# Edge counting with fewer TensorE transposes: x's row tiles 2 to 9 split into halves in rows and turned over by DMA

## The chip, the cores and the metric

The kernel runs as one program on one core of one Trainium2 chip. The metric is device time in microseconds of that core. All inputs start in HBM and the output ends there.

## What is computed

A graph of N = 1250 nodes and E = 41250 edges (`src`, `dst`, sorted by `dst`), node features `x` of 768 values. Three graph layers run one after another; the change touches the first one only. Cut to that layer:

```python
loop = arange(n);  src = concat(src, loop);  dst = concat(dst, loop)
deg = segment_sum(ones, dst)                       # edges into each node, self loop included
norm = rsqrt(deg)[src] * rsqrt(deg)[dst]
h = x @ W                                          # 1250 x 768 by 768 x 768
x = layernorm(x + segment_sum(h[src] * norm[:, None], dst) + b)
```

After it come two attention layers (4 heads of 256, then one head of 768), each with layer norm and a residual product, and a last layer norm.

## The kernel before, in words

**Tiling.** Nodes are cut into T = 10 row tiles of 128 (the last is padded). The program is written out for each engine by hand, with semaphores between them; there is no planner.

**The first layer as matrices.** The kernel doesn't gather edges. It counts them: a 1280 x 1280 matrix C of edge counts (source by destination) is built, and the aggregation is then a matrix product with C. In the same stretch TensorE computes h = x W0, piece by piece between counting blocks. Both factors are kept as a high and a low float16 half (`xt_hi`, `xt_lo`, `w0_hi`, `w0_lo`), and three of the four half products are added, so the product is nearly float32.

**Counting block b (80 of them, WD = 16 destinations each).** VectorE (`one_hots`, L1352) makes two one-hot operands, L1366 and L1367, in ring slot b % 4, so that it can be at most four blocks ahead of TensorE. TensorE (`count_block`, L813) starts the block with one matmul for the self loops (L821) and adds six matmuls (L828); the last of these gives the ring slot back. Then it runs the pieces of x W0 that `pieces_until` puts behind this block: a piece is one 128-wide slice k of one row tile t, and it has six matmuls (L776). From block 18 on there are 43 pieces for 62 blocks, so that 43 blocks have one piece and 19 have none (18, 21, 24, 27, 31, 34, 37, 40, 44, 47, 50, 53, 57, 60, 63, 66, 70, 73, 76). ScalarE copies the block's counts out of PSUM twice (L1103 and, by `cast` at L1068, `c_hi`) once TensorE has started what follows the counting matmuls of that block. After each eighth block TensorE also adds up degrees (`degrees`, L833, matmuls at L839). VectorE has two more steps in every eight blocks: `low_counts` (L1375) after block 8t+6 and the shift of the keys (L1386) after block 8t+4.

**x transposed.** The product needs x with features on partitions. For each row tile, TensorE transposes six 128 x 128 float32 blocks into PSUM buffer `p_out[t % 2]` (`transposes`, L729 to L738), ScalarE casts the result to `xt_hi` (`xt_high`, L1077, its cast at L1068), and VectorE subtracts this from PSUM into `xt_lo` (`xt_low`, L1341, at L1345). Tiles 0 and 1 are done before counting starts, their low half by TensorE and ScalarE too (`less_high`, `xt_rest`). Tiles 2 to 9 are done beside counting, in the blocks that `FETCH` names:

```python
FETCH = {done_block(t) + 2: t + 2 for t in range(T - 2)}
```

which is {13: 2, 19: 3, 28: 4, 37: 5, 45: 6, 54: 7, 63: 8, 71: 9} (block: tile). In such a block TensorE issues the transposes behind the block's pieces (L859), ScalarE casts behind the block's counts (L1105), and VectorE makes the low half after the one-hots of block b + FETCH_LAG, with FETCH_LAG = 4 (L1387). The first piece of tile t comes in block 19, 28, 36, 45, 54, 62, 71 and 79 for t = 2 to 9. The accumulator of tile t is `p_out[t % 2]` as well, so that the transposes wait until the product of tile t - 2 was copied out (`h_read`).

**After the last block.** Five pieces of tile 9 are held back (HELD = 5) and run behind the degrees. VectorE and GpSimd meanwhile turn the degrees into their inverse roots, ScalarE and VectorE scale h (L1116, L1408), and TensorE starts the aggregation (L885). SyncE's queue issued all loads of x and W0 in the first 12 us and then waits for `h_done` (L457) until W1's loads; nothing is on it during counting.

**DMA transposes elsewhere.** L463 (ten, each 128 rows by 1280 float16) and L518 (twenty, each 128 rows by 1024 float16) turn SBUF tiles over by DMA from SyncE's queue.

Of the kernel before, what the change touches and what calls it, by code (L numbers as in the profile page):

```python
# [17 lines left out]
P = 128  # L18
# [31 lines left out]
FETCH_LAG = 4  # L50
# [71 lines left out]
def gnn_program(nc, x, src, dst, W0, b0, W1, a_src1, a_dst1, b1, g1, be1, Wr1, br1,  # L122
# [7 lines left out]
    with ExitStack() as ctx:  # L130
# [102 lines left out]
        w0_lo = at(195 * KB, [KD, D], f16)  # L233
        src_i = at(156 * KB, [EG, P], i32)
# [120 lines left out]
        def everywhere(row):  # L355
# [7 lines left out]
            x_in0 x_in1 x_in2 x_in3 x_in4 x_in5 x_in6 x_in7 x_in8 x_in9 x_tr xt_hi_ok xt_lo_ok h_done h_read hs_hi_ok hs_lo_ok  # L363
# [66 lines left out]
        def _(sp):  # L430
# [18 lines left out]
            for t in range(T):  # L449
                if t == 2:  # L450
                    weights(0)
                if t < T - 1:
                    sp.dma_start(x_sb[:, t, :], x[t * P:(t + 1) * P, :]).then_inc(S[f"x_in{t}"], 16)
                else:
                    sp.wait_ge(S["pads"], 3)
                    sp.dma_start(x_sb[0:LAST, t, :], x[t * P:N, :]).then_inc(S[f"x_in{t}"], 16)
            sp.wait_ge(S["h_done"], T)  # L457
# [252 lines left out]
        def _(pe):  # L710
# [18 lines left out]
            def transposes(t):  # L729

                pe.wait_ge(S[f"x_in{t}"], 16)
                if t >= 2:
                    pe.wait_ge(S["h_read"], t - 1)
                else:
                    pe.wait_ge(S["ident_ok"], 4)
                for k in range(KD):
                    last = pe.transpose(p_out[t % 2][:, k * P:(k + 1) * P], x_sb[:, t, k * P:(k + 1) * P], ident)  # L737
                last.then_inc(S["x_tr"], 1)  # L738
# [63 lines left out]
            def project_nodes(t, k, counted=False):  # L802

                if k == 0:
                    pe.wait_ge(S["xt_lo_ok"], t + 1)
# [42 lines left out]
            for b in range(NB):  # L848
# [10 lines left out]
                if b in FETCH:  # L859
                    transposes(FETCH[b])  # L860
# [205 lines left out]
        def _(act):  # L1066
# [10 lines left out]
            def xt_high(t):  # L1077

                act.wait_ge(S["x_tr"], t + 1 if t < 2 else t + 3)
                cast(xt_hi[:, :, t * P:(t + 1) * P], p_out[t % 2].rearrange("p (k n) -> p k n", k=KD), S["xt_hi_ok"])  # L1080

            def xt_rest(t):

                act.wait_ge(S["x_tr"], t + 3)
                cast(xt_lo[:, :, t * P:(t + 1) * P], p_out[t % 2].rearrange("p (k n) -> p k n", k=KD), S["xt_lo_ok"])

# [12 lines left out]
            for b in range(NB):  # L1099
# [5 lines left out]
                if b in FETCH:  # L1105
                    xt_high(FETCH[b])
# [149 lines left out]
        def _(dve):  # L1256
# [84 lines left out]
            def xt_low(t):  # L1341

                dve.wait_ge(S["xt_hi_ok"], t + 1)
                cols = slice(t * P, (t + 1) * P)
                dve.tensor_tensor(xt_lo[:, :, cols], p_out[t % 2].rearrange("p (k n) -> p k n", k=KD), xt_hi[:, :, cols],  # L1345
                                  ALU.subtract).then_inc(S["xt_lo_ok"], 1)
# [30 lines left out]
            for b in range(NB):  # L1377
# [9 lines left out]
                if b - FETCH_LAG in FETCH:  # L1387
                    xt_low(FETCH[b - FETCH_LAG])
# [465 lines left out]
```

## Time and profile before

| | |
|---|---|
| time, median of 3 runs | 836.49 us (836.45 to 837.44) |
| the profiled execution's own time | 836.33 us |
| its span in the profile | 834.5 us |
| TensorE busy, VectorE busy, ScalarE busy | 807.4, 670.2, 269.2 us |
| mean granted TensorE clock | 0.997 of full speed |

How to read the profile: PE is TensorE's matmuls and PEld its weight loads, DVE is VectorE, ACT ScalarE, POOL GpSimd, SP SyncE; a q behind a name is that engine's sequencer. L828 is line 828 of the kernel. A timeline row has the start in us from the span's start, the time it took, the engine, the line, the operation and, in brackets, the idle time of the engine before it with what ended it. Matmuls overlap: the distance between two starts tells the pace, and the duration of one doesn't. The mean of 16 DMA engines' busy share stands at "DMA".

### The profile page before, as it was taken

What the parts mean: (1) busy time and instruction counts of PE and PEld (TensorE: products, weight loads), DVE (VectorE), ACT (ScalarE), POOL (GpSimd) and SP (SyncE); (2) the same over time, 40 slices, a digit from 0 to 9 for tenths busy, and PEclk for the clock granted to TensorE, in tenths of its full rate; (3) what the DMA queues carried; (4) which work ended last, traced back from release to release, by engine and by line L of the source; (5) the groups of instructions that cost most, each with busy time, mean ns of one, the idle gap of its engine ahead of it and who ended that gap; (6) DMA issues with size and microseconds to landing.
All of it is one profiled execution on the core that took longest, in us unless ns stands there. A gap on an engine that the chain in (4) does not pass through costs nothing.

```text
span 834.5 us, 13407 instructions
## 1 busy us (share of the span) xinstructions
PE 807.4 (97%) x4842; PEld 517.7 (62%) x4842; DVE 670.2 (80%) x1181; ACT 269.2 (32%) x509; POOL 58.8 (7%) x77
## 2 busy tenths in 40 slices
PE   5999999899999999999999999999999999999995
PEld 4566666466454444445888888885555666555552
DVE  7998885778666867998988899978893287996686
ACT  3444434510021101113555556645311108750000
POOL 3000002010203000000000000001111000001111
PEclk9999999999999999999999999999999999999998
DMA  8000002214741266215211322316756432112232
GB/s 309 7 2 2 1 2 70 103 50 157 148 93 70 76 238 225 83 75 207 86 51 50 108 58 89 113 58 143 174 127 157 158 114 76 58 58 76 76 114 72
DMA packets 58829, 82.06 MB, mean 98 GB/s; under 512 B 36997, under 2 KB 37997, under 8 KB 58639
## 3 DMA queue, kind: packets, MB, share of 16 engines
q1 hardware_dynamic: 57502, 76.13, 29.4%
q0 software_dynamic: 1264, 5.11, 1.9%
q8 instruction: 38, 0.62, 0.3%
q14 instruction: 25, 0.20, 0.1%
HBM read 52.40 MB, written 20.31 MB: 87 GB/s over the span
## 4 chain that ended last, share of the span: by engine, by line
PE 83%; DVE 9%; DMA 3%; SPq 2%; issue 2%; DVEq 1%; ACT 1%; POOL 0%; POOLq 0%
PE psum L980 21%; PE psum L962 19%; PE psum L1061 12%; PE psum L885 8%; PE psum L764 8%; DVE arena L1453 6%; PE psum L776 6%; PE psum L828 5%; SPq L463 2%; PE psum L821 1%; PE psum L737 1%; PE psum L992 1%; DMA arena<-as_scratch 1%; PE psum L839 1%; DMA arena<-uv_scratch 1%
## 5 line engine op out<-in xcount | busy, mean ns | idle before, releaser
L980 PE MATMUL psum<-arena 128*128 128x257 f32 x800 | 173.6, 380 | 1.0 <-DVE arena L1599 1.0
L980 PEld LDWEIGHTS psum<-arena 128*128 128x128 f32 x800 | 151.8, 190 | 22.9 <-issue 1.4
L764 PE MATMUL psum<-arena 128*128 128x512 f16 x720 | 158.4, 379 | 2.9 <-DVE arena L1425 1.9
L962 PE MATMUL psum<-arena 128*128 128x512 f16 x960 | 157.4, 326 | 0.0
L1068 ACT ACTIVATE arena<-psum 128x160 f16<-128x160 f32 (+5 forms) x178 | 83.1, 498 | 206.7 <-PE psum L764 73.7
L962 PEld LDWEIGHTS psum<-arena 128*128 128x128 f16 x960 | 93.6, 97 | 62.8
L764 PEld LDWEIGHTS psum<-arena 128*128 128x128 f16 x720 | 69.5, 98 | 88.4 <-issue 7.6
L1068 ACT ACTIVATE arena<-arena 128x1024 f16<-128x1024 f32 (+3 forms) x68 | 56.2, 842 | 135.5 <-DVE arena L1618 47.7
L1061 PE MATMUL psum<-arena 128*128 128x512 f16 (+2 forms) x600 | 98.4, 325 | 0.0
L1061 PEld LDWEIGHTS psum<-arena 128*128 128x128 f16 x600 | 58.3, 97 | 39.8
L1453 DVE CUSTOM_DVE_ANT_0 arena<-arena 128x1280 bf16<-128x1280 bf16 x50 | 71.0, 1489 | 14.9 <-DMA arena<-as_scratch 9.0
L1599 DVE SCALAR_TENSOR_TENSOR arena<-arena 128x640 f32<-128x640 f32 x80 | 65.4, 818 | 14.5 <-ACT arena L1171 12.5
L1171 ACT ACTIVATE arena<-arena 128x640 f32<-128x640 f32 x80 | 64.2, 834 | 37.4 <-DVE arena L1584 37.4
L1584 DVE SCALAR_TENSOR_TENSOR arena<-arena 128x640 f32<-128x640 f32 x80 | 70.1, 879 | 1.4 <-DMA arena<-uv_scratch 1.4
L885 PE MATMUL psum<-arena 128*128 128x512 f16 (+1 forms) x400 | 66.7, 326 | 2.7 <-DVE arena L1408 1.9
L776 PE MATMUL psum<-arena 128*128 128x512 f16 x360 | 68.5, 325 | 0.0
L885 PEld LDWEIGHTS psum<-arena 128*128 x400 | 38.3, 98 | 30.8 <-issue 6.2
L1367 DVE TENSOR_TENSOR arena<-arena 128x960 f16<-128x960 int16 x80 | 52.1, 652 | 0.0
L828 PE MATMUL psum<-arena 128*128 128x160 f16 x480 | 48.3, 235 | 1.8 <-DVE arena L1367 1.8
L1366 DVE TENSOR_TENSOR arena<-arena 128x768 f16<-128x768 int16 x80 | 44.4, 555 | 6.0 <-PE psum L828 2.6
L1463 DVE CUSTOM_DVE_ANT_0 arena<-psum,arena 128x256 bf16<-128x256 f32 x80 | 28.4, 421 | 19.6 <-PE psum L764 19.6
L1103 ACT ACTIVATE arena<-psum 128x160 uint16<-128x160 f32 x80 | 24.4, 305 | 57.6 <-PE psum L776 36.7
(165 smaller groups left out, 684.6 us busy)
## 6 DMA issues: line engine op xcount, KB each, us to landing
arena<-in_L_gnn_W_dram SPq DMA_DIRECT2D x22, 384.0 KB, 3.8
r_scratch<-arena SPq DMA_DIRECT2D x10, 512.0 KB, 2.8
arena<-uv_scratch SPq DMA_DIRECT2D x16, 320.0 KB, 4.4
arena<-r_scratch SPq DMA_DIRECT2D x10, 512.0 KB, 3.9
x_scratch<-arena SPq DMA_DIRECT2D x10, 384.0 KB, 4.6
arena<-x_scratch SPq DMA_DIRECT2D x10, 384.0 KB, 3.6
r_scratch<-arena SPq DMA_DIRECT2D x10, 384.0 KB, 2.7
arena<-r_scratch SPq DMA_DIRECT2D x10, 384.0 KB, 3.9
```

Of the source, the lines that this page charges most:

```text
L764: ins = pe.matmul(o[:, a:b], part[:, k, ds(t * P, P)], w[:, k, a:b], start=(not begun and k == 0 and n == 0 and m == 0), stop=(k == kn - 1 ...
L776: last = pe.matmul(p_out[t % 2][:, a:b], part[:, k, t * P:(t + 1) * P], w[:, k, a:b], start=(k == 0 and name == "hh"), stop=(k == KD - 1 a ...
L828: last = pe.matmul(o, ring_lo[slot][:, i // 2, :, i % 2], ring_key[slot][:, i // 2, :, i % 2], start=False, stop=False, skip_group_check=True)
L885: ins = pe.matmul(p_out[par][:, a:b], counts, part[:, k, a:b], start=(not low and k == 0 and n == 0), stop=(not low and k == T - 1 and n = ...
L962: ins = pe.matmul(o[:, a:b], part[:, k, :], w[k][:, a:b], start=(k == 0 and n == 0 and m == 0), stop=(k == KH - 1 and n == 1))
L980: last = pe.matmul(p_att[:, ATT_BANKS[ch][j], 0:HID + 1], pf[n % PSLOTS][:, j * P:(j + 1) * P], xl[ch % H][:, k, 0:HID + 1], start=(k == 0 ...
L1061: last = pe.matmul(p_att2[c % 2][:, j, a:b], p[n][:, t % C1 * P:(t % C1 + 1) * P], xl2[:, k, a:b], start=(k == 0 and m == 0), stop=(k == T ...
L1068: act.activation(out_, in_, ACT.Copy, scale=scale).then_inc(signal, 1)
L1171: act.activation(ee[s], ee[s], ACT.Exp, bias=as_s[:, ch % H, k:k + 1]).then_inc(S["ex_ok"], 1)
L1453: dve.tensor_tensor_reduce(out=out_, in0=mask, in1=row, scale=1.0, scalar=NEG_BIG, op0=ALU.add, op1=ALU.max, accum_out=mx[:, col, t:t + 1] ...
L1584: dve.scalar_tensor_tensor(ee[s], u_row, asd[:, ch % H, k:k + 1], v_row, ALU.add, ALU.max).then_inc(S["larger_ok"], 1)
L1599: dve.scalar_tensor_tensor(pf[n % PSLOTS], ee[s], 1.0, CT[:, k, ds(ch // H * W1C, W1C)], ALU.min, ALU.mult).then_inc(S["pf_ok"], 1)
```

## The change

It has these parts.

- Tiles 2 to 9 of x are no longer transposed by TensorE. `transposes` is called for tiles 0 and 1 only.
- In the same blocks of `FETCH`, ScalarE (`x_high`) casts the untransposed rows of x from SBUF into a float16 row buffer. Two blocks later (FETCH_LAG = 2 in place of 4) VectorE (`x_low`) subtracts, from SBUF too, and writes the low half into a second row buffer. Both halves have two buffers, `x_rows`, at 180 KB to 186 KB of each partition.
- SyncE's queue, behind the loads of x, waits for each half and issues a DMA transpose of it: 16 transposes of 128 rows by 768 float16, into `xt_hi` and `xt_lo`. They count on `xt_in0` and `xt_in1`, 32 for each tile.
- TensorE waits before the first piece of tile t for `h_read` of tile t - 2 and for both transposes of tile t. ScalarE waits before it writes a row buffer for the transposes of tile t - 2.

```diff
-FETCH_LAG = 4
+FETCH_LAG = 2
...
+        x_rows = [[at((180 + 3 * i) * KB + 1536 * m, [D], f16) for i in range(2)] for m in range(2)]
...
+            for t in range(2, T):
+                for made, rows, to in (("xr_hi_ok", x_rows[0], xt_hi), ("xr_lo_ok", x_rows[1], xt_lo)):
+                    sp.wait_ge(S[made], t - 1)
+                    sp.dma_start_transpose(to[:, :, t * P:(t + 1) * P], rows[t % 2]).then_inc(S[f"xt_in{t % 2}"], 16)
             sp.wait_ge(S["h_done"], T)
...
                 pe.wait_ge(S[f"x_in{t}"], 16)
-                if t >= 2:
-                    pe.wait_ge(S["h_read"], t - 1)
-                else:
-                    pe.wait_ge(S["ident_ok"], 4)
+                pe.wait_ge(S["ident_ok"], 4)
...
                 if k == 0:
-                    pe.wait_ge(S["xt_lo_ok"], t + 1)
+                    pe.wait_ge(S["h_read"], t - 1)
+                    pe.wait_ge(S[f"xt_in{t % 2}"], 32 * (t // 2))
...
-                if b in FETCH:
-                    transposes(FETCH[b])
...
-                act.wait_ge(S["x_tr"], t + 1 if t < 2 else t + 3)
+                act.wait_ge(S["x_tr"], t + 1)
...
+            def x_high(t):
+
+                act.wait_ge(S[f"x_in{t}"], 16)
+                if t >= 4:
+                    act.wait_ge(S[f"xt_in{t % 2}"], 32 * (t // 2 - 1))
+                cast(x_rows[0][t % 2], x_sb[:, t, :], S["xr_hi_ok"])
...
                 if b in FETCH:
-                    xt_high(FETCH[b])
+                    x_high(FETCH[b])
...
-            def xt_low(t):
-
-                dve.wait_ge(S["xt_hi_ok"], t + 1)
-                cols = slice(t * P, (t + 1) * P)
-                dve.tensor_tensor(xt_lo[:, :, cols], p_out[t % 2].rearrange("p (k n) -> p k n", k=KD), xt_hi[:, :, cols],
-                                  ALU.subtract).then_inc(S["xt_lo_ok"], 1)
+            def x_low(t):
+
+                dve.wait_ge(S["xr_hi_ok"], t - 1)
+                dve.tensor_tensor(x_rows[1][t % 2], x_sb[:, t, :], x_rows[0][t % 2], ALU.subtract).then_inc(S["xr_lo_ok"], 1)
...
                 if b - FETCH_LAG in FETCH:
-                    xt_low(FETCH[b - FETCH_LAG])
+                    x_low(FETCH[b - FETCH_LAG])
```

## Rows read from the trace of the kernel before

**Rows 1.** The stretches: time, busy us (and instructions) of each engine, clock, DMA share.

```profile
20.00:40.00 20.00, 18.42 (x146) 10.80 (x144) 20.00 (x37) 10.01 (x34) 0.00 (x0) 1.00 0.07 19
...
120.00:140.00 20.00, 20.00 (x181) 13.15 (x180) 14.62 (x27) 9.10 (x30) 0.00 (x0) 1.00 0.01 2
```

**Rows 2.** Waits, 60 to 140 us for TensorE and 36 to 140 us for VectorE.

```profile
PEld psum L821 <- ACT arena L1068: 9.2, 29, 0.3
...
DVE arena L1345 <- ACT arena L1068: 5.4, 6, 1.3
```

**Rows 3.** TensorE's timeline, blocks 18 to 21, with block 19's transposes.

```profile
46.68 0.24 PE L821 MATMUL psum<-arena 16*128 16x160 f16 x1
46.85 0.60 PE L828 MATMUL psum<-arena 128*128 128x160 f16 x6
47.38 0.24 PE L821 MATMUL psum<-arena 16*128 16x160 f16 x1
...
48.00 1.14 PE L776 MATMUL psum<-arena 128*128 128x512 f16 x6
48.97 0.82 PE L737 MATMUL psum<-arena 128*128 128x128 f32 x6
49.72 0.24 PE L821 MATMUL psum<-arena 16*128 16x160 f16 x1
...
51.41 0.24 PE L821 MATMUL psum<-arena 16*128 16x160 f16 x1
```

**Rows 4.** VectorE's timeline after it made tile 4's low half.

```profile
64.06 0.96 DVE L1345 TENSOR_TENSOR arena<-psum,arena 128x768 f16<-128x768 f32 x1 [0.79 <-ACT arena L1068]
64.93 0.55 DVE L1366 TENSOR_TENSOR arena<-arena 128x768 f16<-128x768 int16 x1
65.40 0.65 DVE L1367 TENSOR_TENSOR arena<-arena 128x960 f16<-128x960 int16 x1
66.39 0.56 DVE L1366 TENSOR_TENSOR arena<-arena 128x768 f16<-128x768 int16 x1 [0.34 <-issue]
```

**Rows 5.** ScalarE's timeline: a block's two copies, and a cast of x behind them.

```profile
116.61 0.30 ACT L1103 ACTIVATE arena<-psum 128x160 uint16<-128x160 f32 x1 [2.27 <-PE psum L821]
116.81 1.00 ACT L1068 ACTIVATE arena<-psum 128x160 f16<-128x160 f32 x2
```

**Rows 6.** Groups of the first 160 us by shape: ScalarE's cast and VectorE's step from SBUF.

```profile
L1068 ACT ACTIVATE arena<-arena 128x768 f16<-128x768 f32 x6 | 4.7, 839 | 0.0
...
L1265 DVE SCALAR_TENSOR_TENSOR arena<-arena 128x768 f16<-128x768 f32 x6 | 5.7, 952 | 0.0
```

**Rows 7.** VectorE's timeline, one-hots of blocks 15 to 17 (tile 2's low half follows).

```profile
39.75 0.82 DVE L1375 TENSOR_TENSOR arena<-arena 128x1280 f16<-128x1280 uint16 x1
40.49 0.55 DVE L1366 TENSOR_TENSOR arena<-arena 128x768 f16<-128x768 int16 x1
...
41.53 0.55 DVE L1366 TENSOR_TENSOR arena<-arena 128x768 f16<-128x768 int16 x1
```

**Rows 8.** The timeline of block 13: TensorE's piece and ScalarE's copies.

```profile
39.38 0.81 PE L776 MATMUL psum<-arena 128*128 128x512 f16 x4
...
39.79 0.30 ACT L1103 ACTIVATE arena<-psum 128x160 uint16<-128x160 f32 x1 [0.86 <-PE psum L776]
```

**Rows 9.** The queue's DMA transposes at L518: issue ns and landing us, min/median/max.

```profile
L518 SPq DMA_TRANSPOSE arena<-arena x20: 1232/1254/2742, 494.0 to 635.6; - x20
...
DMA to landing us min/median/max: 3.0/3.5/5.7
```

**Rows 10.** The same at L463, and the ten of them in the queue's timeline.

```profile
DMA to landing us min/median/max: 3.6/5.1/6.6
...
216.07 18.84 SPq L463 DMA_TRANSPOSE arena<-arena  x10
```

**Rows 11.** TensorE's timeline after the last counting block.

```profile
140.38 1.25 PE L839 MATMUL psum<-arena 128*128 128x1 f16 x40
141.50 5.04 PE L776 MATMUL psum<-arena 128*128 128x512 f16 x30
```

More of the change, by code:

```diff
@@ L362, in gnn_program @@
             keys_ready0 keys_ready1 keys_ready2 keys_ready3 keys_free0 keys_free1 keys_free2 keys_free3 blk_done blk_free
-            x_in0 x_in1 x_in2 x_in3 x_in4 x_in5 x_in6 x_in7 x_in8 x_in9 x_tr xt_hi_ok xt_lo_ok h_done h_read hs_hi_ok hs_lo_ok
+            xr_hi_ok xr_lo_ok xt_in0 xt_in1 x_in0 x_in1 x_in2 x_in3 x_in4 x_in5 x_in6 x_in7 x_in8 x_in9 x_tr xt_hi_ok xt_lo_ok h_done h_read hs_hi_ok hs_lo_ok
             w_in0 w_in1 w_in2 w_in3 w_in4 w_in5 w_hi w_lo clo_ok deg_done dinv_ok over_ok flag_done flag_ok
```

## The prediction

> **What bounds the kernel now.** The change lies in one stage, so I first read the table of stretches for it: during counting, from about 20 to 140 us, which engine is full? Up to 40 us it is VectorE (20.00 of 20 us), and TensorE has gaps (18.42). Late in counting TensorE is busy in all of 20 us, VectorE in 14.62, ScalarE in 9.10 [rows 1]: VectorE sets the pace up to about 40 us, TensorE from there on. The waits say the same: from 60 us on TensorE's only releaser is a gap of 0.3 us before a block's first matmul, put down to ScalarE, and VectorE waits for ScalarE's cast of x, 5.4 us in six waits [rows 2]. The 0.3 us are no work to be saved: the gap is there in blocks of every kind. So from block 18 on time is TensorE's instructions added up, and an instruction less is time less, unless another engine then falls behind.
>
> **What goes.** The pace is read from the starts of L821 in TensorE's timeline [rows 3]. Block 18 (no piece) takes 47.38 - 46.68 = 0.70 us. Block 20 (one piece) takes 51.41 - 49.72 = 1.69, and block 19 (one piece and six transposes) 49.72 - 47.38 = 2.34. The transposes thus cost 0.65 us, less than the 0.82 that their row shows, since matmuls overlap. Eight tiles: 8 x 0.65 = **5.2 us** of TensorE, 0.6% of the kernel. That is the most that the change can bring. The change's waits before a tile's first piece stand in for one that was there, and I cost them at nothing if what they wait for is done; that is checked next.
>
> **What moves.** ScalarE casts x from SBUF, 839 ns [rows 6]. The nearest pair before, a block's last copy and a cast of x from PSUM, takes 1.00 us overlapped [rows 5]; I add 0.03 for the other source, and ScalarE no longer idles until the transposes end. VectorE's subtraction reads SBUF and not PSUM; the nearest row with the same operand types, L1265, takes 952 ns against 956 of L1345 [rows 4, 6]. I take 0.95, and 0.87 until the next start (64.93 - 64.06) [rows 4]. Between those two rows there is no room for more than a few hundredths; what a later finish costs is worked out below.
>
> **Do the transposed halves land in time?** Tile 2 is the tight one, with six blocks from block 13 to 19. ScalarE's copies of block 13 start at 39.79 [rows 8]; a cast behind them ends 116.81 + 1.00 - 116.61 = 1.20 us later [rows 5], so the high half stands at 41.0 and its DMA is issued. VectorE is through with issuing block 15's one-hots at 41.53 [rows 7] (before, block 16's followed there) and subtracts until 42.5. The low half's DMA is issued then, when the first one's 1.25 us of issue are over [rows 9]. Landing takes 3.0 to 5.7 us for 1024 columns [rows 9], 3.6 to 6.6 for 1280 with ten in a row [rows 10]. For 768 columns on an idle DMA (share 0.01) [rows 1] I take 3.1, near the short end. It lands at 45.6. The first piece starts at 48.00 before [rows 3] and 0.65 earlier now, 47.35: 1.7 us to spare. At the long end, 6.6, it lands at 49.1 and costs 1.75 us, once. Later tiles have 8 or 9 blocks. A block takes (43 x 1.69 + 19 x 0.70) / 62 = 1.39 us and 0.07 for degrees, 1.46 in all, so 8 are 11.7 us, of which the casts, the lag and the landing use some 6 to 7. The queue has nothing behind these waits but W1's loads, which wait for the last piece anyway.
>
> **Does VectorE keep ahead?** This is where a price can hide. The subtraction comes two blocks after the fetch block and no longer four, and VectorE is usually four blocks ahead, so it now waits longer for ScalarE (1.3 us at most before [rows 2]; some 2 to 3 us now) and its lead melts. I work out what is left, with 0 at the start (L821) of a fetch block with a piece. The piece starts at 0.61 (48.00 - 47.38 [rows 3]), ScalarE's copies 0.4 later (39.79 - 39.38 [rows 8]), and the cast is done 1.2 + 0.03 after that, at 2.24. VectorE subtracts from 2.27 and is free at 3.14. Its next one-hots are usable after 0.47 + 0.65 [rows 4] and an allowance of 0.06 for the signal, at 4.32, and each block more costs 41.53 - 40.49 = 1.04 [rows 7]. TensorE needs them at the third block's L828, 0.17 behind its start [rows 3]. Degrees take 1.12 / 2 = 0.56 on TensorE [rows 11], `low_counts` 40.49 - 39.75 = 0.74 on VectorE [rows 7]:
>
> - Tile 3 (block 19, with 21 empty): 1.68 + 1.68 + 0.70 + 0.17 = 4.23, so it waits 0.1, and 0.1 again a block later, behind VectorE's `low_counts`.
> - Tile 4 (28): `low_counts` falls in between: 5.06 against 3 x 1.68 + 0.17 = 5.21. Slack 0.15.
> - Tiles 5 and 8 (37, 63, no piece in the block): the first need has slack 0.55, the second, behind an empty block, 0.2.
> - Tiles 6 and 9 (45, 71): 4.32 against 4.8, since degrees fall in between. Slack 0.5. Tile 7 (54): 1.1.
> - Tile 2 (13): VectorE sets the pace here. Its next one-hots are there at 41.53 + 0.87 + 1.18 = 43.6, and TensorE, whose block 16 began at 43.97 before, asks for them 0.65 earlier plus 0.17, at 43.5. Slack 0.
>
> So about 0.2 us of the 5.2 is paid at tile 3, and what comes on top by e at each tile costs the sum of e - slack. Such an e exists: after a wait VectorE's queue has nothing decoded ahead, and block 34's L1366 started 0.42 us late (66.39 - 65.40 - 0.57) with "issue" as the reason [rows 4]. With e = 0.42 everywhere it is 0.42 + 0.42 + 0.27 + 2 x 0.2 = 1.5 us; with none it is nothing. The row is one of six waits of this kind, so I take e = 0.2, half of it: 0.2 + 0.2 + 0.05, some 0.4 us.
>
> **Sum.** 5.2 - 0.2 - 0.4 = 4.6 us off. Behind counting all starts hang on TensorE (held pieces at 141.50) or on the degrees (140.38) [rows 11]; the later stages shift by the same amount, and nothing there is at a fixed time. 836.33 - 4.6 = **831.7 us**. The profiled execution lies 0.16 under the median of the runs; with that it is 831.9, and I give 831.8.
>
> **A rule of the Trainium skill against the change.** The ten transposes of L463, ten blocks of 128 x 128 each, were issued in 18.84 us and landed within 6.6 [rows 10], so at most 1.9 us for ten blocks. "VectorE: DVE Perf Modes", sections "The three transpose paths" and "Rules for kernel authors", has 1309 ns for one 128 x 128 block by DMA against 390 by TensorE and advises TensorE where PSUM will do as a destination. By that, if blocks went one after another, a half would take an estimated 7.9 us, and the estimate by that page would be some 40 us slower. The trace disagrees: its blocks overlap. The sum doesn't use this page.
>
> **Rivals.**
>
> 1. *Tile 2 lands late* (first wait of TensorE for the transposes, 6.6 us landing). For it: the first of a series can be slow, the longest issue was 2.7 us [rows 9]. Against: idle DMA, fewer columns. Costs 1.75: 833.6.
> 2. *VectorE eats the whole gain.* TensorE's transposes go, and waits for L1367 take their place. With the slacks above (sum 2.65) the tiles but the 7th lose 7 x 0.95 - 1.55 = 5.1 us at e = 0.95, with tile 3's 0.2 the whole gain. For: slacks of 0 to 0.2 at five tiles. Against: the gap seen is 0.42 [rows 4], less than half of this. Also here: that the transposes were hidden under the gaps before L821 and their loss shows nothing; block 19's 2.34 us speaks against it. 836.3.
> 3. *Slower: VectorE's lag becomes the bound.* The same place, with e = 1.5 at each tile: 8 x 1.5 - 2.65 + 0.2 - 5.2 = +4.3, 840.6. It decides from e = 0.95 on. For: FETCH_LAG is halved and all of ScalarE's path from a block's end to the cast lies in front of the subtraction. Against: ScalarE is free when it is needed (half busy) [rows 1], and each step is priced from a row.
> 4. *Slower: the transposes run in series.* If each half took its longest landing (6.6) and the low one began when the high one had landed, a pair would need 13.2 us: tile 2 would be 6.8 late, seven tiles by some 2.5 each, 24 - 5 = +19, 855. It decides from about 5 us per half. Against it are the overlapped landings at L463. [...]
>
> **Chances.** Forecast 0.74, rival 1 0.09, rival 2 0.08, rival 3 0.06, rival 4 0.03. The forecast's own bounds: no stall at all, 5.2 off and a few tenths of scatter, 830.7; e = 0.42 everywhere and more of tile 2, 833.5. With rival 1 and part of the way to rival 2 the range is 830.6 to 834.3. No change means within 0.2% (1.7 us), about what a measurement of this kernel can tell. Faster than 834.8 are the forecast, rival 1 and a little of rival 2: 0.84. Same 0.08, slower 0.08.
>
> **What would show it.** L737 with 12 matmuls where it had 60; blocks 19, 28, 45, 54 and 71 at 1.68 us; held pieces starting near 136.9; x_low starting about 2.3 us behind its fetch block's L821, VectorE waiting for ScalarE some 10 us in all; 16 more DMA transposes on the queue landing in about 3 us; TensorE's waits for L1367 after 40 us together under 1 us, in blocks 22, 23, 31 and 41. Wrong would be a wait of TensorE's first pieces for a DMA (rival 1 or 4), or waits for L1367 of 0.7 us in each fetch (rival 2 or 3).

## The result and the profile after

| | before | after |
|---|---|---|
| time, median of 4 runs each, same chip | 836.97 us (836.45 to 837.61) | 831.91 us (831.49 to 832.05) |
| ratio, 95% interval | | 0.9938 (0.9921 to 0.9956) |
| the profiled execution's own time | 836.33 us | 831.99 us |
| its span in the profile | 834.5 us | 830.2 us |
| mean granted TensorE clock | 0.997 | 0.992 |

The change takes 5.1 us off, and the forecast was 831.8. The total is as forecast, but not all of its steps are, and part of the gain comes from where the prediction had none. First the busy times of the page of after, and then the table of stretches (time, busy us and instructions of PE, PEld, DVE, ACT, POOL, then clock, DMA share and GB/s):

```profile
PE 802.7 (97%) x4794; PEld 512.6 (62%) x4794; DVE 670.1 (81%) x1181; ACT 268.7 (32%) x509; POOL 58.7 (7%) x77
```

```profile
20.00:40.00 20.00, 18.63 (x148) 10.93 (x145) 20.00 (x37) 10.18 (x33) 0.00 (x0) 1.00 0.05 13
40.00:60.00 20.00, 19.70 (x193) 12.72 (x191) 19.83 (x37) 9.60 (x32) 0.00 (x0) 1.00 0.29 42
...
120.00:135.00 15.00, 15.00 (x141) 9.77 (x139) 14.14 (x25) 6.52 (x22) 0.00 (x0) 1.00 0.14 28
```

The same last stretch in the trace of before:

```profile
120.00:135.00 15.00, 15.00 (x140) 9.93 (x139) 14.03 (x27) 6.61 (x22) 0.00 (x0) 1.00 0.01 2
```

VectorE and ScalarE do the same work as before within 0.5 us, and TensorE does 4.7 us less. Late in counting TensorE is still full, as in [rows 1]. VectorE is busy for 14.14 of 15.00 us, and for 14.03 of the same 15 us before. The 14.62 of 20.00 in [rows 1], from which the prediction read its slack, include over 4 us behind the last one-hots, in which it idles: VectorE had less room than that row suggests. And the DMA engines, idle before (0.01), are at work. After's lower mean clock comes from a stretch ahead of the change (0.66 from 10 to 20 us, 1.00 in all rows above), and it costs nothing here, as block 13, the first that the change touches, starts at 38.76 to 38.79 us in every profile of this document.

Now TensorE's timeline, around block 19 (to compare with [rows 3]) and at the last counting block, 79:

```profile
46.13 0.24 PE L824 MATMUL psum<-arena 16*128 16x160 f16 x1
...
46.84 0.24 PE L824 MATMUL psum<-arena 16*128 16x160 f16 x1
...
47.46 1.14 PE L778 MATMUL psum<-arena 128*128 128x512 f16 x6
48.53 0.24 PE L824 MATMUL psum<-arena 16*128 16x160 f16 x1
50.22 0.24 PE L824 MATMUL psum<-arena 16*128 16x160 f16 x1
...
135.66 0.24 PE L824 MATMUL psum<-arena 16*128 16x160 f16 x1
...
138.37 5.03 PE L778 MATMUL psum<-arena 128*128 128x512 f16 x30
```

Block 19 lasts 48.53 - 46.84 = 1.69 us where it had 2.34. The first piece of tile 2 starts at 47.46 with no wait before it. Block 79 starts at 135.66, and the pieces that were held back at 138.37, where it was 141.50 [rows 11]. The same line in the trace of before:

```profile
138.79 0.24 PE L821 MATMUL psum<-arena 16*128 16x160 f16 x1
```

So counting is shorter by 138.79 - 135.66 = **3.13 us**, and not by 4.6. I take the start of block 79 as the measure of counting from here on. It repeats well: a second profile of each kernel gave 138.80 and 135.57. Of the 4.34 us between the two profiled executions, 3.13 are counting; 1.2 lie behind it, where the change touches nothing.

Where were the 2.1 us that are missing paid? I compared the length of each block, start of L821 (L824) to the next. The eight fetch blocks lose 0.63 to 0.66 us, 5.2 together. The blocks one to five after a fetch are longer than before, 2.09 us together, 0.93 of it in blocks 66 to 68 alone. TensorE's waits of after, 38 to 136 us (engine, line, releaser: us in all, times, longest), are these, without its weight loads' gaps of 0.3 us before a block's first matmul:

```profile
PE psum L831 <- DVE arena L1373: 0.7, 2, 0.5
PE psum L824 <- issue: 0.4, 1, 0.4
...
PEld psum L831 <- DVE arena L1373: 1.4, 4, 0.7
```

And VectorE's, 36 to 140 us:

```profile
DVE arena L1352 <- ACT arena L1069: 4.7, 4, 2.1
DVE arena L1372 <- issue: 4.1, 12, 0.7
DVE arena L1381 <- ACT arena L1069: 2.3, 1, 2.3
```

The wait at L1381 is behind the last one-hots, at 137 us, and costs nothing. A lesson in reading is here already. The waits for one-hots that the page attributes to VectorE are partly noted on TensorE's weight loads (PEld), so PE's rows alone miss half of them. And VectorE has twelve gaps whose reason is "issue", 4.1 us: nothing that the profile can show ended them. The prediction's e was taken from a gap with this reason. VectorE's timeline behind tile 7's low half shows what they do:

```profile
100.14 0.96 DVE L1352 TENSOR_TENSOR arena<-arena 128x768 f16<-128x768 f32 x1 [0.45 <-ACT arena L1069]
101.02 0.55 DVE L1372 TENSOR_TENSOR arena<-arena 128x768 f16<-128x768 int16 x1
...
102.47 0.56 DVE L1372 TENSOR_TENSOR arena<-arena 128x768 f16<-128x768 int16 x1 [0.33 <-issue]
...
103.92 0.56 DVE L1372 TENSOR_TENSOR arena<-arena 128x768 f16<-128x768 int16 x1 [0.33 <-issue]
...
105.06 0.56 DVE L1372 TENSOR_TENSOR arena<-arena 128x768 f16<-128x768 int16 x1
```

The one-hots of two blocks come at a distance of 1.45 us, and the next at 1.14. The prediction had one late start per fetch, right behind the wait for ScalarE. Here there are two, one and two blocks later, and no wait stands directly before them. So it is another mechanism, and the experiments had to find it.

### The profile page after: what moved, and what is told of

Read it like the earlier page. It is cut to its first block, busy times and chain, and to the rows that moved or that the text cites. A ratio compares the mean times of both kernels' runs of the same rounds, so it can differ in the third digit from the quotient of the medians.

```text
span 830.2 us, 13333 instructions
## 1 busy us (share of the span) xinstructions
PE 802.7 (97%) x4794; PEld 512.6 (62%) x4794; DVE 670.1 (81%) x1181; ACT 268.7 (32%) x509; POOL 58.7 (7%) x77
## 4 chain that ended last, share of the span: by engine, by line
PE 79%; DVE 10%; issue 3%; DMA 3%; SPq 2%; DVEq 2%; POOL 0%; ACT 0%; POOLq 0%
PE psum L981 21%; PE psum L963 19%; PE psum L1062 12%; PE psum L886 8%; PE psum L766 8%; DVE arena L1459 7%; PE psum L778 5%; PE psum L831 4%; SPq L468 2%; PE psum L824 1%; DVEq L1361 1%; PE psum L993 1%; DMA arena<-as_scratch 1%; DVE arena L1373 1%; DMA arena<-uv_scratch 1%
## 5 line engine op out<-in xcount | busy, mean ns | idle before, releaser
L1069 ACT ACTIVATE arena<-psum 128x160 f16<-128x160 f32 (+5 forms) x170 | 76.8, 483 | 201.8 <-PE psum L766 73.7
L1069 ACT ACTIVATE arena<-arena 128x768 f16<-128x768 f32 (+3 forms) x76 | 63.0, 842 | 135.8 <-DVE arena L1624 49.7
L1373 DVE TENSOR_TENSOR arena<-arena 128x960 f16<-128x960 int16 x80 | 52.0, 650 | 0.0
L831 PE MATMUL psum<-arena 128*128 128x160 f16 x480 | 48.3, 235 | 2.2 <-DVE arena L1373 2.0
L1372 DVE TENSOR_TENSOR arena<-arena 128x768 f16<-128x768 int16 x80 | 44.3, 553 | 6.0 <-issue 4.5
```

Of the source, the lines that this page charges most:

```text
L831: last = pe.matmul(o, ring_lo[slot][:, i // 2, :, i % 2], ring_key[slot][:, i // 2, :, i % 2], start=False, stop=False, skip_group_check=True)
L1069: act.activation(out_, in_, ACT.Copy, scale=scale).then_inc(signal, 1)
```

## The experiments

Each kernel below is the changed one with one edit, unless it says otherwise. "Given back" is what block 79's start lies above 133.56, where it starts in the kernel with none of the steps (the first one below).

### None of the steps, and the steps without their DMAs

Two kernels that leave parts of the work out split the price. The first drops all that the change added:

```diff
-                    sp.wait_ge(S[made], t - 1)
-                    sp.dma_start_transpose(to[:, :, t * P:(t + 1) * P], rows[t % 2]).then_inc(S[f"xt_in{t % 2}"], 16)
...
-                        last = pe.matmul(p_out[t % 2][:, a:b], part[:, k, t * P:(t + 1) * P], w[:, k, a:b],
+                        last = pe.matmul(p_out[t % 2][:, a:b], part[:, max(k, 2) if t == T - 1 else k, t % 2 * P:(t % 2 + 1) * P], w[:, k, a:b],
...
-                    pe.wait_ge(S[f"xt_in{t % 2}"], 32 * (t // 2))
+                    pe.wait_ge(S[f"x_in{t}"], 16)
...
-                    x_high(FETCH[b])
...
-                    x_low(FETCH[b - FETCH_LAG])
```

> TensorE's transposes of tiles 2 to 9 are gone and nothing is put in their place: no cast, no subtraction, no DMA; the product of tiles 2 to 9 reads the halves of tiles 0 and 1, so that h is wrong by leaving these tiles' own data out. It measures the ceiling. Theory (eight times 0.655 us of TensorE, nothing else): block 79 starts 5.2 us before 138.79, at 133.6, and the kernel takes 5.2 us less than before. Rival (part of the transposes was hidden under the gap before each block's first matmul): under 4 us.

Measured: block 79 starts at 133.56, 138.79 - 133.56 = 5.23 us earlier than before; median 831.91 us (5 runs) against 837.21 (17 runs), ratio 0.9931 (0.9909 to 0.9953). The saving on TensorE is 8 x 0.654, as read from block 19, and nothing else in counting hides behind it.

The second keeps ScalarE's casts and VectorE's subtractions and drops only the transposes and the waits for them (and reads the same stand-in columns in the pieces as the first):

```diff
-                    sp.wait_ge(S[made], t - 1)
-                    sp.dma_start_transpose(to[:, :, t * P:(t + 1) * P], rows[t % 2]).then_inc(S[f"xt_in{t % 2}"], 16)
...
-                    pe.wait_ge(S[f"xt_in{t % 2}"], 32 * (t // 2))
...
-                    act.wait_ge(S[f"xt_in{t % 2}"], 32 * (t // 2 - 1))
+                    act.wait_ge(S["xr_lo_ok"], t - 3)
```

> The changed kernel without its 16 DMA transposes; cast and subtraction stay, FETCH_LAG = 2, and the product of tiles 2 to 9 reads the halves of tiles 0 and 1 (their own data are left out). Theory A (the 2.1 us given back in the changed kernel's counting come in good part from register loads out of SBUF that take 0.45 to 0.66 us in place of 0.30 while a transpose is in flight, on VectorE's and TensorE's sequencers): all these loads are at 0.30 again, 0.6 to 0.9 us are given back, most of it at block 67, and block 79 starts at 134.2 to 134.5. Rival B (all of it is VectorE's lead, lost to the shorter lag): 2 us are given back as in the changed kernel, block 79 at 135.6.

Measured: block 79 at 134.27, so 0.71 us are given back and not 2.1; 830.73 us (5 runs), ratio 0.9914 (0.9893 to 0.9936). VectorE's timeline at the same place as above, tile 7:

```profile
99.45 0.96 DVE L1347 TENSOR_TENSOR arena<-arena 128x768 f16<-128x768 f32 x1 [1.06 <-ACT arena L1064]
100.33 0.55 DVE L1367 TENSOR_TENSOR arena<-arena 128x768 f16<-128x768 int16 x1
...
101.42 0.56 DVE L1367 TENSOR_TENSOR arena<-arena 128x768 f16<-128x768 int16 x1
...
102.56 0.56 DVE L1367 TENSOR_TENSOR arena<-arena 128x768 f16<-128x768 int16 x1
```

VectorE even waited longer for ScalarE here (1.06 against 0.45), and yet no gap follows. So these gaps do not come from the wait, and the price has two parts at this lag: **0.7 us with casts and subtractions alone, and 1.4 us more with the DMAs in flight**, with nobody waiting for their result. The waits for the DMAs, which this kernel leaves out too, are not what costs: they are all there in a kernel further below (a lag of 4 and loads moved), which gives back 0.06 us.

### What the DMAs slow

The engines' own instructions have the same durations in both kernels (L1372 554 and 552 ns, L1373 650 and 650, TensorE's L831 235 and 235). What differs is in the sequencers. Each block begins, on VectorE and on TensorE, with a load of a register from SBUF (how many rounds the block has). Here are all of them from 36 to 140 us (min/median/max in ns), of before, of after with one load by itself, and of the kernel without DMAs:

```profile
L1355 DVEq TENSOR_LOAD <-arena x65: 297/303/314, 35.8 to 133.1; - x65
...
L816 PEldq TENSOR_LOAD <-arena x68: 293/299/310, 36.5 to 136.3; - x68
```

```profile
L1361 DVEq TENSOR_LOAD <-arena x65: 298/304/656, 35.8 to 132.3; - x65
...
L819 PEldq TENSOR_LOAD <-arena x68: 294/301/656, 36.6 to 133.4; - x68
...
L1361 DVEq TENSOR_LOAD <-arena x1: 656/656/656, 101.3 to 101.3; - x1
```

```profile
L1356 DVEq TENSOR_LOAD <-arena x65: 297/303/314, 35.8 to 130.3; - x65
...
L814 PEldq TENSOR_LOAD <-arena x68: 295/300/311, 36.5 to 131.8; - x68
```

Median and minimum are the same in all three; the maximum is 314 without DMAs and 656 with them. The last row of the middle fence is the load behind tile 7's low half, at 101.3 us: it took 656 ns, and the one-hots behind it started 0.33 us late (102.47 above). In after, 16 of VectorE's 65 loads are longer than 0.4 us, two per tile, and eight of TensorE's 68. All 24 overlap the time from issue to landing of a transpose; 25 more loads overlap one and stay under 0.4 us, and of those that overlap none, none is over 0.314. The engine's queue is empty behind such a load, so the profile can only say "issue". On TensorE the same thing is a gap at a block's start, as behind block 40, which is therefore longer:

```profile
78.44 0.60 PE L831 MATMUL psum<-arena 128*128 128x160 f16 x6
...
79.39 0.22 PE L824 MATMUL psum<-arena 16*128 16x160 f16 x1 [0.35 <-issue]
```

Is it the transposing, or any transfer within SBUF? A kernel that copies the same 128 x 768 halves to the same places:

```diff
-                    sp.dma_start_transpose(to[:, :, t * P:(t + 1) * P], rows[t % 2]).then_inc(S[f"xt_in{t % 2}"], 16)
+                    sp.dma_start(to[:, :, t * P:(t + 1) * P], rows[t % 2].rearrange("p (k n) -> p k n", k=KD)).then_inc(S[f"xt_in{t % 2}"], 16)
```

> The 16 DMA transposes become 16 plain copies of the same rows into the same places (the transposition is left out, so h is wrong). Theory A1 (transposing is what slows register loads): loads stay at 0.30, block 79 as without DMA, 134.2 to 134.5. A2 (any DMA traffic of this size in SBUF slows them): loads of 0.45 to 0.65 us while the copies run, block 79 near 135.5. Rival B (the lead alone): 135.6 with loads at 0.30.

Measured: block 79 at 134.90 (1.34 given back), between the ranges of A1 and A2; 831.58 us (6 runs), ratio 0.9928 (0.9908 to 0.9949). Its register loads:

```profile
L1361 DVEq TENSOR_LOAD <-arena x65: 297/303/636, 35.8 to 131.4; - x65
...
L819 PEldq TENSOR_LOAD <-arena x68: 296/302/623, 36.5 to 132.5; - x68
```

Plain copies lengthen a load nearly as much (636 and 623 against 656), but fewer of them: 14 of VectorE's and 7 of TensorE's are over 0.4 us. So it takes no transposing to slow a load. Copies still cost less, 134.90 - 134.27 = 0.63 of the 1.4 us, and what makes transposes dearer was not separated.

### Lateness, or the loads?

The rivals were tested from the other side too. If the price were in VectorE's lead, giving back the old lag should cure it. If it were TensorE's work being hidden after all (rival 2's second half), putting the transposes back beside the DMAs should cost nothing:

```diff
+                if b in FETCH:
+                    pe.wait_ge(S["h_read"], FETCH[b] - 1)
+                    transposes(FETCH[b])
```

> The changed kernel, with TensorE's transposes of tiles 2 to 9 issued as well at their old places, their results unused. Theory: each costs its 0.655 us again, 5.2 in all, but TensorE then is slow enough for VectorE to keep its lead, so that only the slow register loads on TensorE stay (about 1 us): block 79 at 139.8, kernel 1 us slower than before. Rival (the transposes are partly hidden): block 79 under 138.8.

Measured: block 79 at 140.20, 1.41 above before; 838.51 us (12 runs), ratio 1.0008 (0.9994 to 1.0022). TensorE's fetch block is back at its old length (49.76 - 47.42 = 2.34), and 1.4 us come on top:

```profile
47.42 0.24 PE L824 MATMUL psum<-arena 16*128 16x160 f16 x1
...
49.76 0.24 PE L824 MATMUL psum<-arena 16*128 16x160 f16 x1
```

The rival is refuted. The theory's number was 0.4 us too low, and half of its reason was wrong: blocks 66 and 67 pay 0.8 of the 1.4 us, with a wait for one-hots of 0.7 us, so VectorE did not keep its lead at tile 8. The DMAs and the steps around them have a price even when TensorE is as slow as before. Next, the lag:

```diff
-FETCH_LAG = 2
+FETCH_LAG = 4
```

> The changed kernel with FETCH_LAG = 4 as before. Theory A: VectorE keeps its lead, TensorE's waits for one-hots after block 18 go, the slow register loads on TensorE stay (1 us), and tile 2's halves land at about the time of their need, 0 to 0.5 us late in block 19: block 79 at 134.6 to 135.0. Rival B (all given back is the lead): 133.6 to 134.0. If neither the lag nor the loads matter: 135.6.

Measured: block 79 at 134.52, 0.08 under theory A's range; 831.26 us (6 runs) against 836.70 (11 runs), ratio 0.9933 (0.9919 to 0.9946). Given back: 0.96. VectorE's wait for ScalarE at the low halves (last row) is nearly gone:

```profile
...
DVE arena L1372 <- PE psum L831: 2.7, 6, 0.6
DVE arena L1372 <- issue: 2.4, 9, 0.3
DVE arena L1352 <- ACT arena L1069: 0.9, 2, 0.7
```

The first row shown is the good sign: VectorE now waits for TensorE to free a one-hot buffer, so it is ahead. Its gaps by "issue" are still there and cost little; more than half of what is still given back is in TensorE's own loads (block 40: 0.34, block 55: 0.23). With a lag of 4, tile 2's low half is made two blocks later, and this might cost something of its own. A kernel that keeps the lag of 2 for tile 2 alone:

```diff
-                if b - FETCH_LAG in FETCH:
-                    x_low(FETCH[b - FETCH_LAG])
+                for n in [FETCH[a] for a in FETCH if b == a + (2 if FETCH[a] == 2 else 4)]:
+                    x_low(n)
```

> Lag 2 for tile 2 and 4 for tiles 3 to 9. Theory A: as with 4 throughout, without tile 2's lateness: block 79 at 134.5 to 134.8, the kernel 0.8 to 1.1 us faster than the changed one. Rival B: 133.7, 1.9 us faster.

Measured: block 79 at 134.85; 831.46 us (6 runs), ratio 0.9939 (0.9925 to 0.9953). That is not better than a lag of 4 throughout, 0.33 worse rather: blocks 23 (0.31) and 31 (0.24) pay more. My expectation missed, narrowly by its own range, and an effect of tile 2 being late is not needed to explain the lag of 4. Why the blocks behind tiles 3 and 4 pay more than with a lag of 4 throughout was not looked for.

Then TensorE's loads. Each is issued a block ahead, behind the first matmuls of a piece (or behind the block, where it has none), into one of two registers:

```diff
+            def load_rounds():
+
+                if to_load:
+                    n = to_load.pop()
+                    pe.reg_load(rounds[n % 2], n_groups[0:1, n:n + 1])
...
+                    load_rounds()
...
-                pe.reg_load(rounds, n_groups[0:1, b:b + 1])
-                end = pe.snap(rounds, min_val=1, max_val=ETP // G)
+                end = pe.snap(rounds[b % 2], min_val=1, max_val=ETP // G)
...
+                if b + 1 < NB:
+                    to_load.append(b + 1)
```

> The changed kernel; TensorE's register load of the next block's number of groups (the 0.3 us gap before each block's first matmul) is issued in the middle of a block's piece, or behind the counting matmuls where there is none, into one of two registers. Theory A: the slow loads then lie under queued matmuls, and the 0.1 us that TensorE idles in each block goes too in blocks with a piece: 0.5 to 1.0 us from the slow loads and up to 4 us from 43 to 60 blocks with 0.1 us each; VectorE, at 1.04 to 1.13 us a block, then has less room. Block 79 at 132 to 135. Rival (the gap has another cause, as ScalarE's release or the branch): no change, 135.6.

Measured: block 79 at 135.35; 831.52 us (6 runs), ratio 0.9940 (0.9925 to 0.9955). Alone, this brings only 0.3 us, outside of the theory's range and short of the rival's. Block 40 (-0.09) and block 55 (0.00) are mended, but 0.33 is paid in block 41 in turn and blocks 66 to 68 pay 0.94 as ever: TensorE then waits for VectorE instead. The 0.1 us of idle time before each block's first matmul did not go, and a block with a piece still lasts 1.68.

Two causes, each covered by the other when mended alone; so both together:

```diff
-FETCH_LAG = 2
+FETCH_LAG = 4
...
-                pe.reg_load(rounds, n_groups[0:1, b:b + 1])
+                    pe.reg_load(rounds[n % 2], n_groups[0:1, n:n + 1])
```

> FETCH_LAG = 4 and TensorE's register load of the next block in the middle of a piece, together. Theory: with the lag of 4 alone 0.96 us were given back, of it 0.34 and 0.23 at blocks 40 and 55, where TensorE's load was slow; these two go, the rest stays: block 79 at 133.9 to 134.2, 0.3 to 0.6 us ahead of the lag alone. If the two edits don't add up (VectorE late instead): 134.5 or more.

Measured: block 79 at **133.62**, 0.06 us above the ceiling; 829.54 us (4 runs) against 837.62 (15 runs), ratio **0.9907** (0.9892 to 0.9922). No wait of PE is left from 38 to 136 us. The waits of its weight loads behind the gap at each block's start, and then VectorE's (both without the first row):

```profile
...
PEld psum L832 <- issue: 2.2, 7, 0.3
PEld psum L786 <- issue: 0.3, 1, 0.3
```

```profile
...
DVE arena L1385 <- PE psum L839: 2.4, 6, 0.6
DVE arena L1385 <- issue: 1.9, 7, 0.3
```

VectorE's loads are as long as in after (maximum 660 ns), but it is ahead and they cost nothing. It came out 0.3 us better than the low end that I had expected. The wait at L786 is in block 19, which is 0.17 longer than in the kernel with none of the steps: with a lag of 4, tile 2's low half lands at 47.33, just ahead of its first piece (47.46), and TensorE is idle for 0.27 behind the piece's first matmuls, where its moved load stands. This version, with DMA transposes and all, beats before by 0.9%, and the changed kernel by 2.0 us at block 79; between their ratios, 0.9907 here and 0.9938 and 0.9950 in the two sets of runs of the changed kernel, there is no overlap with the second set and hardly any with the first.

### Tile 8's slack

The largest single payment, 0.93 us in blocks 66 to 68, is more than the DMAs explain: 0.45 of it is there without them. ScalarE's and VectorE's timelines of after at block 63:

```profile
113.18 0.30 ACT L1111 ACTIVATE arena<-psum 128x160 uint16<-128x160 f32 x1 [1.62 <-PE psum L824]
...
113.57 0.84 ACT L1069 ACTIVATE arena<-arena 128x768 f16<-128x768 f32 x1
```

```profile
114.44 0.96 DVE L1352 TENSOR_TENSOR arena<-arena 128x768 f16<-128x768 f32 x1 [2.10 <-ACT arena L1069]
...
116.76 0.56 DVE L1372 TENSOR_TENSOR arena<-arena 128x768 f16<-128x768 int16 x1 [0.32 <-issue]
...
118.58 0.56 DVE L1372 TENSOR_TENSOR arena<-arena 128x768 f16<-128x768 int16 x1 [0.69 <-issue]
```

Block 63 starts at 111.72. It has no piece, so ScalarE's copies follow the next block's first matmul, and between the two TensorE counts a tile's degrees, 0.5 us. The subtraction thus starts 2.72 us behind the block's start, where the other tiles have 2.24 to 2.44 (the first tile, in the stretch that VectorE bounds, 2.76). The prediction had used 2.27 for it and a slack of 0.2.

The last row shows something else: the second gap is 0.69 us and not 0.33. Without DMAs there is a gap at the same one-hots too:

```profile
117.03 0.56 DVE L1367 TENSOR_TENSOR arena<-arena 128x768 f16<-128x768 int16 x1 [0.38 <-issue]
```

In the instructions of VectorE's sequencer, every kernel of this document, before and the one with none of the steps too, has five places from 36 to 138 us where nothing happens for 0.40 to 0.44 us between two of them (in before at 65.66, 82.34, 98.78, 118.16 and 133.65 us). In before no wait and no slow load stands there. In 44 of these 65 cases the next packet of the DMA engines' instruction queue follows 1.1 to 1.2 us later; that points at the loading of code, but no run tests it. One of the five falls on tile 8 in both kernels, and how much of its price is this and how much the degrees is open. One block earlier the degrees are not in the way:

```diff
-FETCH = {done_block(t) + 2: t + 2 for t in range(T - 2)}
+FETCH = {done_block(t) + (1 if t == 6 else 2): t + 2 for t in range(T - 2)}
```

> The changed kernel with tile 8 fetched in block 62 in place of 63. In block 63 ScalarE's copies wait for the first matmul of block 64, and the degrees (0.57 us) lie before it, since block 63 has no piece; the prediction's slack for tile 8 left that out. Theory: the 0.93 us given back in blocks 66 to 68 fall to 0.3 or less, block 79 at 134.8 to 135.1. Rival (VectorE is late there through the slow register loads alone): at least 0.6 us are given back in blocks 64 to 68 as before, 135.3 or more.

Measured: block 79 at 134.73, 0.07 better than expected at the low end; blocks 64 to 68 pay 0.13 in place of 0.93; 831.71 us (4 runs), ratio 0.9936 (0.9919 to 0.9952). VectorE waits 1.00 us for tile 8 instead of 2.10, and the gap of 0.38 is still there (117.49) with room behind it:

```profile
112.23 0.96 DVE L1352 TENSOR_TENSOR arena<-arena 128x768 f16<-128x768 f32 x1 [1.00 <-ACT arena L1069]
```

### Each kernel once more

> The changed kernel once more, for the spread. Block 79 at 135.66 within 0.2 us, with two slow register loads of VectorE for each tile at the same places. The part of the span behind it was 694.54 in the first profile and 695.71 in that of before; if this 1.2 us is a matter of when DMAs of the attention stage land, it comes out anywhere between.

The changed kernel: block 79 at 135.57, two slow loads of VectorE for each tile (up to 670 ns) at the same places, 694.88 us behind block 79's start; 832.82 us (6 runs) against 836.70 (11 runs), ratio 0.9950 (0.9936 to 0.9963).

> The kernel before once more. Block 79 at 138.8 within 0.1 us, no register load over 0.4 us from 36 to 140 us. From block 79 to the end it took 695.71 in the first profile, the changed kernel 694.54 and 694.83. If the 1 us between them is chance in the landing of the attention stage's DMAs, this one lies between 694 and 697; if the change does something there, within 0.2 us of 695.7.

The kernel before: block 79 at 138.80, no load over 315 ns, 694.84 us behind; 836.73 us (11 runs) against 837.62 (15 runs), ratio 0.9996 (0.9986 to 1.0006). The median of one and the same kernel thus moves by 0.9 us, which is more than most of the effects above; only the position of block 79 resolves them.

What the blocks behind each tile's fetch are longer than before (us), and the two measures (TensorE's transposes put back is left out, since its fetch blocks are not shorter; it pays 0.3 behind tile 5, 0.2 behind 6, 0.1 behind 7 and 0.8 behind 8). The first row, the next three, the three from "lag 4" and the last two were measured in four sets, each beside before in the same set: compare ratios across sets, not medians.

| kernel | t2 | t3 | t4 | t5 | t6 | t7 | t8 | block 79 | median | ratio |
|---|---|---|---|---|---|---|---|---|---|---|
| after | .10 | .41 | .06 | .32 | .05 | .22 | .93 | 135.66 | 831.91 | 0.9938 |
| nothing added | 0 | 0 | 0 | 0 | 0 | 0 | 0 | 133.56 | 831.91 | 0.9931 |
| no DMAs | .08 | .18 | 0 | 0 | 0 | 0 | .45 | 134.27 | 830.73 | 0.9914 |
| plain copies | .12 | .20 | 0 | .14 | 0 | .05 | .75 | 134.90 | 831.58 | 0.9928 |
| lag 4 | .10 | .14 | .11 | .34 | 0 | .23 | 0 | 134.52 | 831.26 | 0.9933 |
| lag 2 at tile 2, else 4 | .11 | .41 | .24 | .33 | 0 | .22 | 0 | 134.85 | 831.46 | 0.9939 |
| loads early | .24 | .13 | .16 | .24 | 0 | 0 | .94 | 135.35 | 831.52 | 0.9940 |
| lag 4, loads early | .16 | -.06 | 0 | -.09 | 0 | 0 | 0 | 133.62 | 829.54 | 0.9907 |
| tile 8 in block 62 | .11 | .34 | .05 | .33 | 0 | .20 | .13 | 134.73 | 831.71 | 0.9936 |

Differences under 0.05 us per block are left out, so a row's sum can be 0.1 off its block 79. The 0.16 of "lag 4, loads early" is block 19, tile 2's first piece. No kernel pays anything at tile 9.

## Why the prediction came true, and where it did not

**What bounds the kernel, and what goes.** Right, and exactly so: 5.2 us were worked out from block 19, and the kernel with nothing added shows 5.23. Rival 2's second half (transposes hidden under the gaps) is refuted twice, by that kernel and by the one with TensorE's transposes put back.

**What moves.** Right: the cast takes 0.84 us, the subtraction 0.95 to 0.96, and VectorE's start after a fetch block's start is 2.24 to 2.44 us for tiles 3 to 7 and 9, with 2.27 forecast. Wrong: VectorE waits for ScalarE 4.7 us at the low halves, where I had said some 10. It was not four blocks ahead everywhere: at tiles 3 and 6 it came to the subtraction after the cast was done.

**Do the halves land in time?** Right. Tile 2's transposes were issued at 41.06 and 42.5 us, and all sixteen landed early:

```profile
L461 SPq DMA_TRANSPOSE arena<-arena x16: 1210/1250/1316, 41.1 to 127.2; - x16
...
DMA to landing us min/median/max: 2.7/2.8/4.5
```

I had taken 3.1 us near the short end of 3.0 to 6.6. The nearest rows had ten transposes in a row or other columns on a busier DMA; pairs on idle engines land at the short end and a little below it. Rivals 1 and 4 are refuted. (What the prediction said for rival 1, that the first of a series can be slow, its row does not show: the issues of 2.2 to 2.7 us at L518 are each the second of a pair.) The Trainium skill, page "VectorE: DVE Perf Modes", section "The three transpose paths", gives 1309 ns for one 128 x 128 block by DMA; six one after another would be an estimated 7.9 us by that page. The measurement decides against such a sum: six blocks were issued in 1.25 us and landed in 2.8 together. The advice in the same page's section "Rules for kernel authors", to transpose on TensorE where PSUM will do, does not hold in this stage, which TensorE bounds: with the DMA transposes it is 3.1 us shorter.

**Does VectorE keep ahead?** This is the step that failed. It had 0.2 + 0.4 = 0.6 us for what is paid back, and 2.1 us were. Its sign, TensorE's waits for one-hots (L1373 now) together under 1 us, failed too: they are 1.4 us, in blocks 22, 23, 67 and 68. Three parts of it:

- *The size and the place of e.* I had read "issue" as a queue that has nothing decoded after a wait, once per tile, and took half of 0.42 us. Most of the gaps are a register load of 0.30 us that takes up to 0.66 while a transfer within SBUF is in flight. It comes twice per tile (two gaps of 0.33), and it depends on the DMAs, not on the wait. The row it was taken from [rows 4] is of a kernel that has no such DMAs in that stage, and its loads never exceed 314 ns: that gap is one of the five standstills of the sequencer (65.66 us), which come in every kernel. The number was near, the mechanism was not, and so it was put in once where it belonged twice.
- *An engine left out.* TensorE has such loads too, one per block. It pays directly, in blocks 40 and 55 (0.32 and 0.22), where VectorE's slack plays no part. Tile 7 had the greatest slack (1.1) and pays nevertheless.
- *Tile 8's slack.* 0.2 was worked out for "tiles 5 and 8" together. For tile 8 the degrees lie between the empty block and ScalarE's copies, and nearly half a microsecond of slack was not there (2.72 - 2.24). One of the sequencer's standstills falls there as well. It pays 0.93 of the 2.09; moving it by one block takes this down to 0.13.

Tile 3 pays 0.41 us as forecast (0.2 and 0.2), but partly for another reason: without DMAs it pays 0.18.

**The sum.** 5.23 - 2.09 = 3.14 us come off in counting, and 4.6 had been forecast. Held pieces start at 138.37, not at 136.9. The stages behind do not simply shift: from block 79's start to the end of the execution's time, before needs 836.33 - 138.79 = 697.5 us and after 831.99 - 135.66 = 696.3. This 1.2 us made up for most of what the counting stage lacked. So **the total was met in part by luck**, and the forecast's case (some 0.6 paid) did not occur as written; it was a third of the way from it to rival 2 (5.2 paid). Rivals 2 and 3 named the right place, VectorE's lag, with prices that were too high.

**What stays open** is this 1.2 us. The two traces differ where a small array (`uv_scratch`) goes through DRAM and back ahead of attention (engine, line, releaser: us, times, longest), first before and then after:

```profile
DVE arena L1584 <- DMA arena<-uv_scratch: 1.4, 1, 1.4
```

```profile
DVE arena L1590 <- DMA arena<-uv_scratch: 0.6, 1, 0.6
```

Chance is one reading: in the repeats both kernels have 696.7 us behind block 79 (835.45 - 138.80 and 832.25 - 135.57), and medians of the same kernel differ by 0.9. But chance is not shown to be all of it. From the issue of the array's store to the end of the span, the two profiles of before need 458.1 and 458.0 us, and the two of after 457.3 and 457.3; what lies between block 79 and the store scatters both ways (237.6 and 236.9 against 237.2 and 237.6). The store itself lands after 4.4, 4.2 and 4.8 us in the two profiles of before and in the kernel with TensorE's transposes put back, after 3.8 with none of the steps, and after 3.0 to 3.6 in the nine others. In the first three, and in no other, a packet of the instruction queue (16 KB) moves within 0.4 us of the store's issue. TensorE's instructions are more in these kernels, so its code may be loaded at other times; that is an argument, and no run tested it. The medians less block 79's start part in nearly the same way: 697.9 to 698.8 us for before in each set, the kernel with none of the steps and the one with the transposes put back, against 695.9 to 697.3 for the others. The kernel with none of the steps fits only half. From the medians' 5.1 us, then, 3.1 are explained by counting and up to 2 are not; the repeat of the changed kernel has 3.9, with 3.2 in counting. The kernel with both mendings has 8.1, with 5.2 in counting.

## What to carry to other kernels

When work moves from the bounding engine to a helper that must stay ahead, work the lead out for every place on its own, with what stands between the trigger and the helper's first instruction there; two places that look alike (tiles 5 and 8) differed by a tile's degrees. Then look at what the moved work shares with everybody else: here transfers that nobody waited for lengthened small loads of a register from SBUF on the sequencers of both engines that had such loads, so issue such loads a step ahead where the bounding engine has other work queued. Two faults that cover each other show little when they are mended singly (1.1 and 0.3 us here), and everything together (2.0).

## What the hardware showed that was not expected

- A register load from SBUF takes 0.30 us (0.293 to 0.315 in every kernel without transfers within SBUF), and up to 0.656 us on both VectorE's and TensorE's sequencers in after while a DMA transpose is in flight (0.670 and 0.685 at most in the other kernels); a plain copy within SBUF of the same size does nearly the same (0.636 and 0.623 us). The profile shows it only as "issue" on the engine behind it.
- A DMA transpose of 128 x 768 (two bytes per element) within SBUF, issued on an otherwise idle queue in 1.25 us, landed 2.7 to 4.5 us after its issue, 2.8 at the median.
- With these transfers, sixteen of 128 x 768, the stage of some 100 us lost 1.4 us on engines that never waited for them; with VectorE's lag of 4 and TensorE's loads moved, it lost less than 0.1.
- VectorE's sequencer stands still for 0.40 to 0.44 us at five places from 36 to 138 us in all thirteen profiles, with or without DMAs; where VectorE has nothing queued, the page shows it as "issue" too.
